# A gated recurrence and eight experts in one kernel: statistics of the next x moved behind the levels, gathers issued ahead of scatters, and the second expert product in rounded parts from tile 12 on

## What is computed

```
x = x + attn(layernorm(x))
    q = silu(x@wq); k = sigmoid(x@wk); v = x@wv; f = 1 - k; theta = cumsum(sign(f-0.5))*pi
    S_t = S_{t-1}*f_t + k_t v_t^T ; out_t = q_t S_t        (2 heads, rotated by theta)
    out = layernorm(out * sigmoid(x@wg1@wg2)) * norm_w @ wo
x = x + ffn(layernorm(x))
    e = argmax(x @ centroids.T), one of 8 experts; alpha = sigmoid(best affinity)
    h = relu(layernorm_e(x) @ w1[e].T + b1[e]);  y_e = x + h @ w2[e].T + b2[e]
    out = alpha*y_e + (1-alpha)*x
```

## Time and profile before

| | us |
|---|---|
| median of 3 runs | 653.22 (652.31 to 654.06) |
| the profiled execution | 650.17 |
| its span, first to last instruction | 648.4 |

### The profile page before, as it was taken

One profiled execution on the slowest core, in us unless ns is written; L12 is line 12 of the kernel. 1 busy time (PEld: TensorE's weight loads), 2 busy tenths in 40 slices (PEclk: granted clock), 3 DMA queues, 4 the chain that ended last, 5 costly groups with the idle time before them and its releaser, 6 DMA issues.

```text
span 648.4 us, 12299 instructions
## 1 busy us (share of the span) xinstructions
PE 593.3 (92%) x3638; PEld 501.8 (77%) x3639; DVE 346.1 (53%) x941; ACT 281.5 (43%) x679; POOL 260.8 (40%) x390
## 2 busy tenths in 40 slices
PE   3888999899999999997789979999999999999991
PEld 2556677686877768776789969988899999998981
DVE  2196895959689695998743354222233322332230
ACT  3454556767665775755352412222222223222220
POOL 7715153553918455463433251332222332233311
PEclk9898999999999999996989999999999999999997
DMA  9910010110403011111696573655554565555200
GB/s 323 407 36 32 2 65 1 66 66 3 131 1 99 1 65 33 67 33 49 173 357 195 179 244 99 222 188 190 192 176 178 186 217 202 176 182 187 112 21 1
DMA packets 25188, 83.60 MB, mean 129 GB/s; under 512 B 3822, under 2 KB 13424, under 8 KB 18993
## 3 DMA queue, kind: packets, MB, share of 16 engines
q1 hardware_dynamic: 16896, 59.57, 26.6%
q0 software_dynamic: 7552, 22.89, 10.4%
q10 hardware_dynamic: 688, 0.52, 0.3%
HBM read 70.35 MB, written 13.53 MB: 129 GB/s over the span
## 4 chain that ended last, share of the span: by engine, by line
PE 76%; DVE 10%; issue 4%; POOL 3%; DMA 3%; ACT 1%; DVEq 0%; ACTq 0%; POOLq 0%
PE bank_l L1176 20%; PE bank_a L1160 19%; PE bank_a L936 7%; PE bank_l L924 6%; PE bank_a L965 5%; DVE arena L1250 4%; PE bank_c L1039 3%; DMA arena<-rows_by_expert,take_idx 2%; PE bank_b L1016 2%; DVE arena L1261 2%; PE bank_a L981 2%; PE bank_a L974 2%; PE bank_b L1015 2%; PE bank_c L1056 2%; PE bank_b L1002 2%
## 5 line engine op out<-in xcount | busy, mean ns | idle before, releaser
L1160 PEld LDWEIGHTS bank_a<-masks,arena 128*128 128x128 f32 x1248 | 146.5, 194 | 1.7
L1548 DVE TENSOR_TENSOR arena<-bank_a,b_col 128x512 f32<-128x512 f32 x78 | 53.9, 691 | 175.6 <-PE bank_a L1160 161.8
L1160 PE MATMUL bank_a<-masks,arena 128*128 128x128 f32 x1248 | 147.2, 277 | 0.0
L1176 PE MATMUL bank_l<-w_sb,arena 128*128 x624 | 143.4, 383 | 4.0 <-issue 3.0
L1176 PEld LDWEIGHTS bank_l<-w_sb,arena 128*128 128x128 f32 x624 | 116.5, 192 | 20.7 <-issue 6.4
L670 POOL DMA_INDIRECT out<-k_mix,put_of x39 | 41.1, 1055 | 178.8 <-DVE k_mix L1562 172.3
L924 PEld LDWEIGHTS bank_l<-arena,k_mix 128*128 128x128 f32 x448 | 65.5, 198 | 45.8 <-ACT k_mix L705 33.4
L880 ACT ACTIVATE arena<-arena 128x512 f32<-128x512 f32 x78 | 44.9, 622 | 106.2 <-PE bank_l L1176 104.6
L1250 DVE TENSOR_TENSOR arena<-arena 128x256 f32<-128x256 f32 x224 | 88.2, 437 | 5.1 <-PE bank_l L924 5.0
L924 PE MATMUL bank_l<-arena,k_mix 128*128 128x128 f32 x448 | 73.5, 290 | 12.4 <-DVE arena L1261 10.6
L936 PE MATMUL bank_a<-arena 128*128 128x512 f32 x160 | 82.0, 612 | 0.0
(11 more groups left out here) (150 smaller groups left out, 771.0 us busy)
## 6 DMA issues: line engine op xcount, KB each, us to landing
arena<-w SPq DMA_DIRECT2D x39, 1024.0 KB, 4.8
arena<-x SPq DMA_DIRECT2D x16, 512.0 KB, 5.6
w_sb<-w SPq DMA_DIRECT2D x8, 1024.0 KB, 14.3
arena<-b SPq DMA_DIRECT2D x1, 1024.0 KB, 14.1
arena<-rows_by_expert,take_idx POOLq DMA_INDIRECT x39, 3.7
out<-k_mix,put_of POOLq DMA_INDIRECT x39, 4.1
rows_by_expert<-arena POOLq DMA_INDIRECT x32, 4.8
arena<-wk SPq DMA_DIRECT2D x1, 256.0 KB, 3.9
```

The source lines that it names most:

```text
L1160: m = pe.matmul(bank_a[k // 4][:, k % 4 * P:(k % 4 + 1) * P], w1_now[t.par][:, i * F + k * P:i * F + (k + 1) * P], xl_t[t.par % 2][:, i * ...
L1176: m = pe.matmul(bank_l[p][:, 0:D], h_act[:, k * P:(k + 1) * P], w2_sb[:, bass.ds(e * (FC * D) + k * D, D)], start=(k == 0), stop=(k == FC ...
L1548: dve.tensor_tensor(h_sb[:, n * 512:(n + 1) * 512].rearrange("p (k t) -> p k t", t=P), bank_a[n][:, :].rearrange("p (k t) -> p k t", t=P), ...
```

## The change

It has four parts.

1. **Second product in rounded parts, tiles 12 to 38.** w2[e] is split into w2_high (rounded to the type float32r) and w2_low = w2 - w2_high, and relu(h) into h_high and h_low in the same way. The product becomes h_high w2_high + h_high w2_low + h_low w2_high, 24 matrix products instead of 8. ScalarE makes w2_high of tile t+1 at the end of its turn(t) (`high_part`); VectorE makes w2_low at the start of its turn and h_low at the end.
2. **GpSimd.** In a turn the gather for tile t+4 now stands ahead of the scatter of tile t; four turns instead of three stand ahead of the last sequence's row scatter.
3. **The next x.** Its statistics on VectorE move from between levels 2 and 3 to behind the states; GpSimd's norm of it moves to just ahead of the product of q for level 0; ScalarE's x_norm moves behind the gates, ahead of mixing level 0.
4. **Levels 5 and 6** are picked by ScalarE with six plain copies of whole blocks (`wide_pick`) instead of four predicated copies on VectorE.

The core of the diff:

```diff
             def turn(n):
+                target(n)
+                if n + SLOTS < TILES:
+                    pool.wait_ge(s_put, n + 1)
+                    gather(n + SLOTS)
                 scatter(n)
-                if n + SLOTS < TILES:
-                    gather(n + SLOTS)
...
-            for n in range(3):
+            for n in range(4):
                 turn(n)
             scatter_rows(LAST_SEQ)
...
+            def wide_pick(b, l):
+
+                h = 2 ** l
+                need(act, s_lev, H * LEVELS, b, H * l + H)
+                if l == MASKED:
+                    need(act, s_at0, H, b, H)
+                for odd in range(2):
+                    for n in range(HALF // h):
+                        p0 = (2 * n + odd) * h
+                        scores = bank_l[l % 2][p0:p0 + h, :].rearrange("p (m two s) -> p m two s", m=PAIRS, two=2)[:, :, odd, n * h:(n + 1) * h]
+                        copy(strided(attn_t[b.par][p0:p0 + h, :], (P if odd else h) + n * 2 * h, [2 * P, PAIRS], [1, h]), scores).then_inc(s_wide, 1)
...
-                of(nxt, x_norm)
+                of(b, wide_pick, 5)
                 of(a, q_sigmoid, 1)
+                of(b, wide_pick, 6)
                 of(b, k_tok_copies)
...
                 of(a, gate_sigmoid, 1)
 
+                of(nxt, x_norm)
                 of(a, mix, 0, 0)
...
+            def high_part(t):
+                e = act.value_load(expert_of(t), min_val=0, max_val=E - 1)
...
+                need(act, s_ye, 1, before(t, 2), 1)
+                copy(w2_high[t.par % 2], w2_of(e)).then_inc(s_whi, 1)
+
             def turn(t):
                 relu(t)
                 if exists(before(t, -2)):
                     gains(before(t, -2))
+                if exists(before(t, -1)) and in_parts(before(t, -1)):
+                    high_part(before(t, -1))
...
+            def down_in_parts(t):
+
+                p = t.par % 2
+                need(pe, s_yb, 1, before(t, 2), 1)
+                need(pe, s_whi, 1, t, 1)
+                need(pe, s_wlo, 1, t, 1)
+                for k in range(FC):
+                    if k % 4 == 0:
+                        need(pe, s_hr, 2, t, k // 4 + 1)
+                    h, w = slice(k * P, (k + 1) * P), slice(k * D, (k + 1) * D)
+                    pe.matmul(bank_l[p][:, 0:D], h_high[:, h], w2_high[p][:, w], start=(k == 0), stop=False)
+                    pe.matmul(bank_l[p][:, 0:D], h_high[:, h], w2_low[p][:, w], start=False, stop=False)
+                for k in range(FC):
+                    if k % 4 == 0:
+                        need(pe, s_hlo, 2, t, k // 4 + 1)
+                    m = pe.matmul(bank_l[p][:, 0:D], h_low[:, k * P:(k + 1) * P], w2_high[p][:, k * D:(k + 1) * D],
+                                  start=False, stop=(k == FC - 1))
+                m.then_inc(s_ye, 1)
...
-                of(nxt, x_stats)
                 level(3)
...
-                of(b, pick, 6)
...
                 of(b, states)
+                of(nxt, x_stats)
...
+            def w2_low_part(t):
+                e = dve.value_load(expert_of(t), min_val=0, max_val=E - 1)
+                need(dve, s_whi, 1, t, 1)
+                dve.tensor_tensor(w2_low[t.par % 2], w2_of(e), w2_high[t.par % 2], ALU.subtract).then_inc(s_wlo, 1)
+
+            def h_low_part(t, n):
+                need(dve, s_ye, 1, t, 0)
+                need(dve, s_hb, 2, t, n + 1)
+                need(dve, s_hr, 2, t, n + 1)
+                w = slice(n * 512, (n + 1) * 512)
+                dve.scalar_tensor_tensor(out=h_low[:, w], in0=h_sb[:, w], scalar=0.0, in1=h_high[:, w],
+                                         op0=ALU.max, op1=ALU.subtract).then_inc(s_hlo, 1)
+
             def turn(t):
                 one = before(t, -1) if exists(before(t, -1)) else None
+                if one is not None and in_parts(one):
+                    w2_low_part(one)
+                    finish(before(t, 1))
+                    bias_h(one, 0)
+                    bias_h(one, 1)
+                    h_low_part(one, 0)
+                    h_low_part(one, 1)
+                    return
```

More of the change, by code:

```diff
@@ L95, in build_program @@
     LEVELS = 7
+    MASKED = 5
     HALF = P // 2
@@ L122, in build_program @@
         ARENA = 33808
-        arena_at = nc.sbuf_base
+        arena_at = -(-nc.sbuf_base // 32) * 32
         arena = sb("arena", [P, ARENA], F32)
+        assert nc.sbuf_base == arena_at + 4 * ARENA
         class Layout:
@@ L184, in build_program @@
         h_act = lay3.take(F)
+        h_at = lay3.at - F
+        lay3.at = dead_at - F
+        h_low = lay3.take_rounded("h_low", F)
+        h_high = nc.alloc_sbuf_tensor_at("h_high", [P, F], F32R, offset=arena_at + 4 * h_at)[:, :]
+        lay4 = Layout(dead_at, PHASE1_AB)
+        w2_high = [lay4.take_rounded(f"w2_high{i}", FC * D) for i in range(2)]
+        w2_low = [lay4.take_rounded(f"w2_low{i}", FC * D) for i in range(2)]
         earlier = lay2.take(P)
@@ L207, in build_program @@
         k_mix = [sb(f"k_mix{i}", [P, PAIRS * P], F32)[:, :] for i in range(2)]
-        b2_sb = lay3.take(E * D)
+        b2_sb = arena[:, h_at + F:h_at + F + E * D]
+        assert h_at + F + E * D <= dead_at - F
         ident = sb("ident", [P, P], F32)
@@ L297, in build_program @@
         s_pick = sem("level_picked")
+        s_wide = sem("wide_levels_picked")
         s_k7 = sem("k_transposed")
@@ L332, in build_program @@
         s_hr = sem("h_ready")
+        s_whi = sem("w2_high_ready")
+        s_wlo = sem("w2_low_ready")
+        s_hlo = sem("h_low_ready")
         s_ye = sem("y_done")
@@ L460, in rounds, with in_parts, w2_of @@
                 turn(Step(i // SLOTS, i % SLOTS, SLOTS))
+        def in_parts(t):
+            return not isinstance(t.half, int) or number(t) >= NA
+        def w2_of(e):
+            return w2_sb[:, bass.ds(e * (FC * D), FC * D)]
         def exists(t):
@@ L615, in step @@
                     norm("o", c)
-                if nxt is not None:
-                    need(pool, s_xn, TJ, nxt, 0)
-                    norm("x", nxt)
                 if c is not None and number(c) > 0:
@@ L651, in step @@
                     norm("o", b)
+                if nxt is not None:
+                    need(pool, s_xn, TJ, nxt, 0)
+                    norm("x", nxt)
                 if a is not None:
@@ L662, in gather, with target @@
                                         in_offset=bass.IndirectOffsetOnAxis(ap=take_idx[:, n:n + 1], axis=0)).then_inc(s_rows[p], 16)
-            def scatter(n):
+            def target(n):
                 p = n % SLOTS
@@ L667, in scatter @@
                 pool.tensor_scalar(put_of[:, n:n + 1], gathered[p][:, 2 * D + 1:2 * D + 2], skip[:, n:n + 1], None, ALU.add).then_inc(s_put, 1)
+            def scatter(n):
+                p = n % SLOTS
                 pool.wait_ge(s_put, n + 1)
@@ L683, in _ @@
             double_norm(LAST_SEQ)
-            for n in range(3):
+            for n in range(4):
                 turn(n)
             scatter_rows(LAST_SEQ)
-            for n in range(3, NA - SLOTS):
+            for n in range(4, NA - SLOTS):
                 turn(n)
@@ L879, in relu @@
                     w = slice(i * F // 2, (i + 1) * F // 2)
-                    act.activation(h_act[:, w], h_sb[:, w], ACT.Relu).then_inc(s_hr, 1)
+                    act.activation((h_high if in_parts(t) else h_act)[:, w], h_sb[:, w], ACT.Relu).then_inc(s_hr, 1)
+            def high_part(t):
+                e = act.value_load(expert_of(t), min_val=0, max_val=E - 1)
+                if isinstance(t.half, int) and number(t) in (NA, NA + 1):
+                    need(act, s_o, 2, LAST_SEQ, 2)
+                    need(act, s_og, 2, LAST_SEQ, 2)
+                need(act, s_ye, 1, before(t, 2), 1)
+                copy(w2_high[t.par % 2], w2_of(e)).then_inc(s_whi, 1)
             def turn(t):
@@ L890, in _ @@
             act.wait_ge(s_small, 64)
-            need(act, s_pick, 2 * LEVELS, LAST_SEQ, 2 * LEVELS)
+            act.sem_inc(s_whi, 1 + NA)
+            need(act, s_pick, 2 * MASKED, LAST_SEQ, 2 * MASKED)
             gains(tile(0))
@@ L919, in level @@
                 need(pe, s_mix, 2 * H * LEVELS, b, 2 * (H * l + h + 1))
-                need(pe, s_pick, 2 * LEVELS, b, 2 * max(l - 1, 0))
+                if l <= MASKED + 1:
+                    need(pe, s_pick, 2 * MASKED, b, 2 * max(l - 1, 0))
                 for m in range(h * PAIRS // H, (h + 1) * PAIRS // H):
@@ L1006, in outputs @@
             def outputs(b, half, between=None):
-                need(pe, s_pick, 2 * LEVELS, b, 2 * LEVELS)
+                need(pe, s_pick, 2 * MASKED, b, 2 * MASKED)
+                need(pe, s_wide, 6, b, 6)
                 need(pe, s_state, 5, b, 5)
@@ L1184, in turn @@
                     z_transposes(before(t, -2))
-                down(t)
+                if in_parts(t):
+                    down_in_parts(t)
+                else:
+                    down(t)
             pe.wait_ge(s_const, 1)
```

(5 more changed lines are left out.)

6 lines of the change are left out of this document (3 added, 3 removed).

## The result

The changed kernel takes 795.26 us (median of 4 runs, 794.35 to 796.52), the kernel before 652.76 (4 runs, 652.19 to 654.06): a ratio of 1.218, with a 95% interval of 1.216 to 1.221. The profiled execution took 794.35 us and has a span of 792.6 us. 798 had been forecast, with 780 to 815 as the likeliest range.

A forecast was written before the change was run, and what follows sets the result against it. TensorE, busy 92% of 648.4 us, was taken to bound the kernel. Second stage +159.4, GpSimd -6.5 and levels -7.5 made +145.4 on 650.17: 795.6, plus 3 for the median, 798 us; likeliest 780 to 815 (0.54), whole range 748 to 848.

The forecast's parts named there:

- The ring: Tiles 12 to 38: first product, transposes, gains, copy, subtraction, finish, bias, next first product; 11.85 us at full clock, not 7.42.
- the one sign missed: TensorE's waits for predicated copies should fall from 10.6 us to 3 or less.
- The clock: Tiles 13 to 38: TensorE's hole lowers the clock for the next first product, 1.7 us a tile, making 13.55 us.
- The second product: 24 rounded products per tile on TensorE take 2.7 to 5.2 us, all hidden.
- The rival with 10.6 us: Rounded products on TensorE no faster than full ones, 14.6 us a tile without a hole; 826 us, chance 0.06.
- clock stays up: Rival for tiles 12 to 38: 11.85 us a tile with no clock lost; 754 us, chance 0.15.
- whole first product at 1.2 GHz: Rival for tiles 12 to 38: clock down for the whole first product, 15.4 us a tile; 847 us, chance 0.17.
- GpSimd: Earlier gather removes tile 7's 4.52 us wait for rows and the clock loss behind it; -6.5 us, ends 0 and -6.7.
- the earlier gathers buy nothing: In tiles other than 7 no gather is waited for, so going 1.3 us earlier gains nothing.
- The levels: First stage: TensorE gets back part of 12.5 us of waits for VectorE; -7.5 us, ends -12.5 and +3.
- the price that had been set for x_norm's move: ScalarE's x norm, 2.06 us, ahead of mixing level 0: 0.3 us over its hole, 0.3 to 0.5 in seven steps.
- not slower: Rival: copy and subtraction don't hold the bias, VectorE's 7.1 us a tile is the limit; 631 us, chance 0.05.

The follow-up runs named there:

- the kernel with the filled hole: The changed kernel with each second product from tile 12 done twice plus three unused products of ident and w2 behind it: 747.6 us, ratio 1.150.
- the kernel with the copy first: The changed kernel with ScalarE's copy of w2 ahead of the gains, VectorE's order as changed: 652.14 us, ratio 1.001.
- both parts alone: The kernel before with the move of the next x and the block picks of levels 5 and 6, without GpSimd's part: 639.76 us, ratio 0.986.
- part 1 alone: The kernel before with only the second product in rounded parts for tiles 12 to 38: 811.33 us, ratio 1.243.
- GpSimd's part alone: The kernel before with only the new GpSimd order, gathers ahead of scatters: 644.18 us, ratio 0.989.
- the block picks alone: The kernel before with only levels 5 and 6 picked by ScalarE: 653.14 us, ratio 1.003.
- the biases first: The changed kernel with VectorE's turn reordered to bias, finish, bias, then the subtraction and low parts of h: 619.65 us, ratio 0.951.
- the kernel with the product done twice: The changed kernel with the 24 products of each tile from 12 on done twice into the same bank: 769.95 us, ratio 1.182.

## Why the prediction was right, point by point

The profiled execution had been summed to 795.6 us; it took 794.35. The parts: +159.4 in the 26 intervals (measured 161.5), -14 ahead of them (-18.3), 0 behind them (+1.0). The mechanism, the ring with part of the clock lost, is the one that the runs show. That the sum came within 1.3 us is luck in part, since errors of opposite sign stand in it: 2.1 and 1.0 us too little, 4.3 too much.

**The ring** stood as forecast, link by link, and so did its signs (the one sign missed, 5.1 us of waits for predicated copies where 3 or less had been forecast, belongs to the levels): the bias as TensorE's largest wait (4.6 us each, forecast about 5), the subtraction waiting for the copy and starting 9.2 us behind a first product (forecast 7.2 and the clock's 1.7). Two terms were mis-sized, and they nearly cancel:
- At full clock the ring was put at 11.85 us. Its links measure: to the transposes 5.78 (3.57 at full clock), to the gains 0.55, to the copy 0.81, to the subtraction 2.06, to finish 2.21, to the bias 1.30, to the next first product 0.75. With 3.57 for the first link that is 11.25; the kernel with the filled hole shows 11.33 in the turn above and 11.54 in the mean, so the surplus was 0.3 to 0.6 us. It lay in issue time: 0.38 for ScalarE's load of the expert number, which does not appear (the copy starts as the gains end, 512.82 + 0.81 = 513.63), and 0.22 ahead of finish, which does not either. Both engines have these loads in their streams, here behind a long operation or a long wait. The 0.38 came from a place between two short operations on VectorE, and the 0.36 ahead of the bias, of which that is still true, is there. That the operation or wait ahead is what hides the load is an inference from these three places; no run varied it.
- The clock was put at 1.7 us a tile and costs 5.78 - 3.57 = 2.2 here (13.63 - 11.54 = 2.1 in the mean). The 1.7 came from work of 4.98 us behind a hole, part of which (the transposes) was short; in the ring the first product is at 1.2 GHz for its first 4.5 us.

The estimates from columns held: the copy of 2048 columns had been put at 1.87 us from 512 and 128 columns, the subtraction at 2.29 from 512 and 256. By the groups (line, operation, shape, count, busy us, mean ns of one):

```profile
L1645 DVE TENSOR_TENSOR w_low<-w_sb,w_high 128x2048 fp32r<-128x2048 f32 x27 | 61.9, 2293 | 186.8 <-ACT w_high L732 186.8
L732 ACT ACTIVATE w_high<-w_sb 128x2048 fp32r x27 | 51.7, 1915 | 1.8 <-issue 1.6
L1245 PE MATMUL bank_l<-w_high,h_high 128*128 128x256 f32 x216 | 53.8, 290 | 0.8 <-ACT h_high L921 0.8
...
L1250 PE MATMUL bank_l<-w_high,h_low 128*128 128x256 f32 x216 | 30.2, 282 | 0.0
```

**The second product** is one record a product, spaced 0.12 us (from 512.41 to 514.32 are 16 steps of 0.119), 2.8 us for 24: the low end of the range of 2.7 to 5.2. Before it was 3.5 for 8 products. The Trainium skill (FP8 and Floating Point Precision, TensorE Precision Notes) has full float32 as four passes; that a rounded operand needs one is not said there in words, the prediction read it from that, for an estimate of 2.6 us. The trace agrees with the reading: 0.119 us for a rounded product, 0.44 for a full one (3.5 us for 8). The rival with 10.6 us is out.

**The clock.** Here filling the hole brought 44 us of 795 back, between 5 and 6%, with work added. The Trainium skill (TensorE: Matmul & The Clock Gate, What's actually happening) puts the ramp penalty at less than 1% of a typical kernel's span. This kernel, which stops and starts TensorE in every tile, is not covered by that figure, and the prediction was right to take its own hole instead.

**The rival "clock stays up"** had pointed to the hole of 0.54 us without loss. That observation is right, and the filled kernel confirms it for 0.8 us and the kernel with the copy first for 1.4, but the holes of this kernel are 4.4 to 5.2 us. **The rival "whole first product at 1.2 GHz"** would have cost 3.57 us a tile, and 2.2 were lost: 4.5 of the 5.8 us are at the lower clock.

**GpSimd:** -6.5 forecast, -7.4 alone. The wait of tile 7 is gone but for 0.2 us, as forecast. At its own place this term was too large: 4.2 us are gained around tile 7. The step that was wrong beside it is that the earlier gathers buy nothing in the other tiles: from tile 12 on they go with 2.6 us. The two nearly cancel.

**The levels:** -7.5 forecast, -9.2 for both parts alone, and -12.4 in the profiled executions (the first product of tile 1 starts at 322.82 instead of 335.20). The 12.4 are at the far end: in the six profiles with the changed first stage tile 1 starts at 322.8 to 329.5, in the mean at 326.7, and in the three with the old one (the kernel before, part 1 alone, GpSimd's part alone) at 335.2 to 336.7, 335.8 in the mean. That is 9 us, as the ratio has it. Of the 12.4 the waits account for 5.8: picks 10.6 to 5.1, the product of q 1.9 to none, keys on ScalarE 1.2 up to 2.8. What the prediction's step left out is what follows a wait. Two stretches of TensorE at the start, before:

```profile
20.00:30.00 10.00, 8.08 (x25) 5.45 (x24) 1.52 (x3) 3.96 (x9) 8.42 (x11) 0.83 1.00 414
...
50.00:60.00 10.00, 8.78 (x39) 6.00 (x40) 7.71 (x20) 5.27 (x13) 6.47 (x9) 0.83 0.16 52
```

and after:

```profile
20.00:30.00 10.00, 10.00 (x36) 6.16 (x35) 4.31 (x12) 4.83 (x9) 7.58 (x13) 1.00 1.00 415
...
50.00:60.00 10.00, 9.56 (x47) 6.98 (x46) 5.76 (x17) 4.43 (x9) 6.71 (x12) 1.00 0.00 0
```

A mean of 0.83 over ten us is 3.4 us at 1.2 GHz, in which half the work is lost, 1.7 us. In the first stretch stood the wait of 1.92 us for a product of q. It is 1.92 and 1.93 us in GpSimd's part alone and in the block picks alone too, and the clock falls behind it there as well; in part 1 alone it is 1.27 us, and the clock stays up:

```profile
20.00:30.00 10.00, 8.73 (x33) 5.53 (x31) 1.92 (x3) 5.62 (x11) 8.18 (x11) 1.00 1.01 417
```

So these 1.7 us go with the wait, and the prediction, which had charged such a loss for the new holes, had not credited it for this old one. For the second stretch the same can't be said. The kernel with the copy first has the changed first stage, and its profile shows the same loss twice:

```profile
30.00:40.00 10.00, 8.48 (x40) 6.28 (x39) 7.54 (x13) 6.04 (x18) 1.68 (x1) 0.83 0.46 152
45.00:55.00 10.00, 8.18 (x34) 5.38 (x33) 9.24 (x20) 5.41 (x18) 3.68 (x8) 0.83 0.00 0
```

Whether the clock falls there differs from execution to execution, so this loss can't be put down to the change. A steady step is 36.5 us instead of 37.3, part of which are the shorter waits; the price that had been set for x_norm's move, 0.3 to 0.5 us a step, doesn't show.

**The rival "not slower"** had put the kernel at 631 us if the ring were open, by 7.1 us of VectorE's work a tile. With the biases first it is open, and the kernel is at 620: the tile takes 6.6 to 6.7 us, since the issue times that are in the 7.1 mostly don't show there, and TensorE's own work is as long.

## What to carry to other kernels

When work is added ahead of an operation in an in-order queue, look for the way from that operation back to the new work's own input: here the addition of a bias waited for a copy that waited for the product which waited for the bias, and no engine was busy throughout. The cure was the same work in another place, behind the operation that others wait for: 0.951 instead of 1.218 by another order of the same calls and one more semaphore wait. A hole on TensorE of 1.8 to 2.3 us cost here its length and in most cases 1.6 us of clock behind it, one of 4.4 to 5.2 us 2.1 to 2.2 us, so a wait can be worth more than its own row says, when it comes and when it goes.

## What the runs showed that was not expected

- More work on TensorE made the kernel faster twice: 2.8 us a tile more in the second product gave 24 us back, and three spare products on top of that another 21 (ratios 1.218, 1.182, 1.150).
- In the kernel with the product done twice, holes of 1.61 to 1.77 us left the next first product at 3.8 us (one of 14 such took 5.5), and behind holes of 1.78 to 2.27 us it took 5.4 to 5.5 in ten of eleven; behind holes of 4.4 to 5.2 us in the changed kernel it takes 5.8 to 6.1. What decides besides the length of the hole stays open.
- The start of tile 12 differs by 7 us between the profiles of six kernels with the same first stage and the same order on GpSimd (411.67 to 418.78), so a single pair of profiles doesn't fix a gain of that size in the first stage.
- A product with rounded operands of 256 columns is one record, 0.12 us after the one before; a full one is two records and takes 0.44 us.
